# A macaron layer (MoE feed-forward, attention, MoE feed-forward): router banks and the order of scores and value matmuls

## The reference, cut to what matters

```
# feed-forward: 16 routed experts (width 256), all computed densely, and 2 shared ones (width 512)
logits = flat @ router_w                      # 2048 x 16
probs = softmax(logits); weights, idx = top_k(probs, 2); weights /= weights.sum()
comb = sum(one_hot(idx, 16) * weights[..., None], axis=1)
h = silu(flat @ wg_r) * (flat @ wu_r) * comb
out = shared(flat) + einsum('tem,emd->td', h, wd_r)
# attention: 16 heads of 64, with a bias that depends on the relative position
k, v, q = split(x @ w_in, 3)
weights = softmax(q k^T / 8 + bias(rel))
out = (weights v) @ w_gate + b_gate;  return a * sigmoid(g)     # a, g = split(out)
```

## Time and profile before

| what | us |
|---|---|
| two timed runs | 3918.69 and 4110.19 |
| their median, the time before | 4014.44 |
| the profiled execution's own time | 3800.72 |
| its span on the slowest core (core 1) | 3799.1 |
| spans of the eight cores | 3731.9 to 3799.1 |
| TensorE busy | 2845.7 |
| VectorE busy | 1138.8 |
| ScalarE busy | 967.3 |

### The profile page before, as it was taken

The page is one execution under the profiler, slowest core; times in us unless marked ns, Lnnn a source line. Parts: engine busy times, 40 slices in busy tenths (PEclk is TensorE's granted clock), DMA queues, the critical chain, the costliest instruction groups (busy, mean ns, idle before and its releaser), DMA issues. The chain is left out here.

```text
span 3799.1 us, 36293 instructions; the slowest of 8 cores (3731.9 to 3799.1 us)
## 1 busy us (share of the span) xinstructions
PE 2845.7 (75%) x12680; PEld 1215.2 (32%) x12680; DVE 1138.8 (30%) x2460; ACT 967.3 (25%) x987; POOL 172.7 (5%) x265
## 2 busy tenths in 40 slices
PE   0354768999999376767667677656449999999996
PEld 0122324444444222222222222223224444444443
DVE  2521102213031433533534434422433022130320
ACT  2200001101010244645645546531121011010110
POOL 0001110000000001001000001010000000000000
PEclk9577889999999678778778777779859988999888
DMA  3269978556574233223233323222118454564545
GB/s 113 35 114 171 179 171 189 152 170 189 136 180 138 44 48 62 57 53 60 52 54 53 58 46 60 44 33 23 11 42 193 139 158 130 152 186 146 153 127 172
DMA packets 207456, 407.86 MB, mean 107 GB/s; under 512 B 59904, under 2 KB 109312, under 8 KB 207120
## 3 DMA queue, kind: packets, MB, share of 16 engines
q1 hardware_dynamic: 96080, 316.24, 29.8%
q0 software_dynamic: 101968, 52.61, 13.2%
q10 hardware_dynamic: 9232, 36.70, 3.3%
HBM read 405.00 MB, written 40.37 MB: 117 GB/s over the span
## 5 line engine op out<-in xcount | busy, mean ns | idle before, releaser
L560 PE MATMUL f_p<-hf,f_wgu 128*128 128x512 bf16 x2560 | 630.6, 403 | 120.5 <-DMA f_wgu<-wu_r 86.1
L637 PE MATMUL f_p<-f_pall,f_wdb 128*128 128x512 bf16 x2560 | 571.8, 387 | 51.8 <-DMA f_wdb<-wd_r 29.2
L571 PE MATMUL f_p<-hf,f_wgu 128*128 128x512 bf16 x2560 | 607.6, 393 | 0.0
L1098 ACT ACTIVATE at_pexp<-at_ps,at_ngm 128x1024 bf16<-128x1024 f32 x512 | 530.0, 1111 | 181.3 <-PE at_ps L1066 174.0
L1118 DVE TENSOR_TENSOR at_pt<-at_pexp,at_e 128x512 bf16<-128x512 bf16 x1024 | 382.1, 421 | 363.7 <-ACT at_pexp L1098 203.8
L591 ACT ACTIVATE f_gs<-f_p 128x1024 bf16<-128x1024 f32 x160 | 163.7, 1023 | 1110.1 <-PE f_p L560 1110.1
L1046 PE MATMUL at_ppr<-at_pt,at_vtm 128*65 128x512 bf16 x1024 | 372.7, 504 | 83.9 <-DVE at_pt L1118 83.8
L560 PEld LDWEIGHTS f_p<-hf,f_wgu 128*128 128x128 bf16 x2560 | 261.2, 103 | 465.0 <-issue 252.7
L599 DVE TENSOR_TENSOR f_t<-f_p,f_bc 128x1024 f32<-128x1024 f32 x128 | 156.8, 1225 | 740.0 <-PE f_p L571 740.0
L637 PEld LDWEIGHTS f_p<-f_pall,f_wdb 128*128 128x128 bf16 x2560 | 253.1, 99 | 370.7 <-issue 82.3
L571 PEld LDWEIGHTS f_p<-hf,f_wgu 128*128 128x128 bf16 x2560 | 257.1, 100 | 323.8 <-issue 93.5
(11 more groups left out here) (106 smaller groups left out, 1369.6 us busy)
## 6 DMA issues: line engine op xcount, KB each, us to landing
f_wgu<-wbf_scr SPq DMA_DIRECT2D x140, 1024.0 KB, 6.6
f_wdb<-wbf_scr SPq DMA_DIRECT2D x140, 512.0 KB, 3.8
f_bc<-comb_scr SPq DMA_DIRECT2D x128, 256.0 KB, 7.3
wbf_scr<-f_wgu SPq DMA_DIRECT2D x20, 1024.0 KB, 7.6
at_e<-etab_scr SPq DMA_DIRECT2D x32, 608.0 KB, 4.5
at_e<-etab_scr ACTq DMA_DIRECT2D x32, 608.0 KB, 4.5
wbf_scr<-f_wdb SPq DMA_DIRECT2D x20, 512.0 KB, 4.0
xt<-x ACTq DMA_DIRECT2D x1, 8192.0 KB, 39.4
```

Of the source, the lines that this page charges most:

```text
L560: pg=pg, tb=tb: h.matmul(pg[:, mc * 512: mc * 512 + 512], wgu[buf][:, c * 256 + mc * 128: c * 256 + mc * 128 + 128], hf[:, c * S + tb * TB ...
L571: pu=pu, tb=tb: h.matmul(pu[:, mc * 512: mc * 512 + 512], wgu[buf][:, 2048 + c * 256 + mc * 128: 2048 + c * 256 + mc * 128 + 128], hf[:, c ...
L637: mc=mc, po=po, col=col, u=u: h.matmul(po[:, col: col + 512], wdb[buf][:, mc * 1024 + dch * 128: mc * 1024 + dch * 128 + 128], p_all[:, u ...
L1098: hh=h_: h.activation(out=pexp[:, (q % 2) * 2048 + half_i * 1024: (q % 2) * 2048 + half_i * 1024 + 1024], in_=p_s[:, half_i * 1024: half_i ...
```

## The change

In the router the single accumulator becomes four: tile `t` uses bank `t % 4` of `P[0]` and `P[1]`, with columns shifted by 16 for each round of four. The wait of TensorE is then for the copy that was made four tiles earlier in that bank. In attention PV(q-1) is issued behind S(q) for q = 1, 2, 3, and PV(3) alone at the end. `flush_a` stays behind S(1), so PV(0) comes behind it.

```diff
-                ev_prev = None
+                ev_cp = [None] * 4
                 for t in range(NT):
-                    if ev_prev is not None:
-                        ph.wait("tensor", ev_prev)
+                    bk = t % 4
+                    pb = P[bk // 2]
+                    sl = (bk % 2) * 512 + (t // 4) * 16
+                    ph.wait("tensor", ev_cp[bk])
...
-                            P[0][:, 0:16],
+                            pb[:, sl: sl + 16],
...
                                 if q == 1:
                                     flush_a()
-                                if q == 2:
-                                    emit_pv(0)
-                                    emit_pv(1)
+                                if q >= 1:
+                                    emit_pv(q - 1)
...
-                            emit_pv(2)
                             emit_pv(3)
                             flush_b()
```

More of the change, by code:

```diff
@@ L392, in ffn_phase @@
                 pre_issued = first_call
-                ev_prev = None
+                ev_cp = [None] * 4
                 for t in range(NT):
-                    if ev_prev is not None:
-                        ph.wait("tensor", ev_prev)
+                    bk = t % 4
+                    pb = P[bk // 2]
+                    sl = (bk % 2) * 512 + (t // 4) * 16
+                    ph.wait("tensor", ev_cp[bk])
                     for c in range(NDCH):
-                        ph.op("tensor", lambda h, t=t, c=c: h.matmul(
-                            P[0][:, 0:16],
+                        ph.op("tensor", lambda h, t=t, c=c, sl=sl, pb=pb: h.matmul(
+                            pb[:, sl: sl + 16],
                             hf[:, c * S + t * 128: c * S + t * 128 + 128],
@@ L406, in ffn_phase @@
                     ph.wait("vector", ev_mm)
-                    ev_prev = ph.op("vector", lambda h, t=t: h.tensor_copy(
-                        out=lg[:, t * 16: t * 16 + 16], in_=P[0][:, 0:16]),
+                    ev_cp[bk] = ph.op(
+                        "vector", lambda h, t=t, sl=sl, pb=pb: h.tensor_copy(
+                            out=lg[:, t * 16: t * 16 + 16], in_=pb[:, sl: sl + 16]),
                         inc="v")
```

## The result

The changed kernel takes 3686.58 us (median of 11 runs), the kernel before 3779.74 (median of 10, the two of the table above among them). Some executions of either are longer because the cores of one die show a lower clock; they are left out of the ratio, which is 0.977 with a 95% interval of 0.972 to 0.983: 86 us of 3780, between 65 and 106 (so it isn't settled on which side of 2% it lies). The forecast was a gain of 70 us and a time of 3944, between 3830 and 4025. The gain lies in the interval, the time far outside its range. The changed kernel's profiled execution took 3678.8, the old one's 3800.7.

A forecast was written before the change was run, and what follows sets the result against it. No engine is full in attention; a chain of waits sets the pace. Attention 61.6 us, less 5 for the division's trip, plus router 13, gave 70 us off the 4014.4 median: 3944, range 3830 to 4025.

The forecast's parts named there:

- first rival, Full clock through the middle: Attention's clock stays full mid-cycle: early half 11.0 us a cycle, late half 12.4; 116 us saved, 3898; chance 0.15.
- Attention: New PV order: mean cycle 12.43 us against 13.3, 61.6 us saved; some 57 shorter with 5 charged for the division's trip.
- full-clock cycle: Attention cycle laid out at full clock: 0.7 us idle before exp(2)A, no gap before exp(3)A, 11.0 us.
- half-clock cycle: Attention cycle laid out at half clock: 1.7 us idle before exp(2)A, 0.5 before exp(3)A, 12.6 us.
- The mix: Attention: two cycles in three at half clock until S(3) (12.6 us), one with clock up during PV(1) (12.1); mean 12.43.
- Round trip: Attention's division (reciprocal, store, broadcast load, multiplication) becomes level with the shorter cycle late in attention; 5 us charged.
- Router: Both router calls: with four banks a tile takes 0.35 us instead of 0.787; 13 us saved, between 0 and 17.
- All cycles at half clock: Attention cycles all 12.6 us, first ones 12.0, and only 5 us from the router: 50 us saved, 3964; chance 0.17.
- The rule that was weighed there: Skill rule: short pauses between matmul groups make the clock alternate, losing throughput; by it all new attention cycles could be half clock.
- The slower case: Attention: the `at_e` load shares DMA engines with the broadcast load and prolongs the division's trip; +16 us, 4030; chance 0.08.

The follow-up runs named there:

- filled: Changed kernel plus six useless matmuls a cycle (4 behind S(0), 2 ahead of PV(3)); ratio to the kernel before 0.962, attention 1070.8 us.
- div_late: Changed kernel with `flush_b` moved from behind mult(3) to behind mult(0) of the next cycle; ratio to the kernel before 0.974, attention 1119.4 us.
- early_tr: Changed kernel with `flush_a` behind S(0) instead of S(1), `flush_b` behind mult(0) of the cycle after; ratio to the kernel before 0.960, attention 1064.7 us.

## Why the prediction was right or wrong

**The time (wrong).** The step that failed is the sentence "I take the same 70 off the median: 4014.4 - 70 = 3944", and the range behind it. Two runs 190 us apart are no base: eight more of the same kernel lie at 3753 to 3900, and with them the median is 3779.74, 235 us lower. The profiled execution had said so: 3800.7. The sum against that, 3731, is 1.2% from what was measured (3687); the range did not even include it. Nor does the range follow from its own words: half the distance of the two runs is 96 us, and 3898 less 96 and 4005 plus 96 would be 3802 to 4101, which misses 3687 as well. With the profiled time as base the first rival's 116 us would have led to 3685, near what was measured.

**The gain (right in size, in part by luck).** 70 forecast, 65 to 106 measured. The mechanism was right, a long gap before exp(3) traded for a shorter one before exp(2), but errors of its terms offset each other:

- *Attention, 57 for 65.7.* The gap before exp(3) went and a smaller one came before exp(2), as laid out. The full-clock cycle was forecast at 11.0 and is 10.98 (in its sum 4.74 + 2.04 is 6.78 and not 6.76, which changes nothing). The half-clock cycle was forecast at 12.6 and is 13.09: I had counted four PV as 4 x 0.43 = 1.72, and from PV(0) to S(2)A they take 1.85, and again before S(3)A. That is half of the 0.49; in the cycle shown PV(1) also comes 0.97 behind S(2)A where I had 0.86, and I had taken 12.6 for a sum of 12.67. The mix made up for it, and that is luck: I had two cycles in three at half clock until S(3) and none at full, but only 11 to 16 of 56 on a core are 13.0 to 13.4 long and 5 to 12 take 11.0, and the mean is 12.22 instead of 12.43.
- *Round trip, 5 for 14.* The mechanism was right, and VectorE's waits for `at_bca` grew, from 115 to 174 us on the slowest cores. Wrong was its rule of place: I had it bind late in attention, where the trip was 10 us, and said that the late half can't go to 11.0. That was read from core 1; on cores 2, 3, 6 and 7 of the same execution the mean trip is 8.3, early and late. In the changed kernel 10.98 stands in late groups too, and the held cycle shown above is in the third group.
- *Router, 13 for 17.8.* The spacing of 8 matmuls behind a wait (0.22) was the right end of the bound: 0.226. The forecast 0.35 was too careful. The estimate by the Trainium skill ("TensorE: Matmul & The Clock Gate", section "Wait — 56ns, not 53.3ns?"), 62 ns a matmul, is not what these rows show: 28 ns with all the loads of weights between them, at a granted clock of 0.50.

**The rivals.** Full clock through the middle did not come about by the change. Its full-clock cycle of 11.0 was priced right, and filled, where most cycles have it, shows attention 63 us shorter than the changed kernel's. That the late half would be held at 12.4 then was wrong: div_late and early_tr take the hold away, and filled has cycles of 11.0 late as well. All cycles at half clock fell, too: the clock rose from 0.77 to 0.84. The rule that was weighed there (the Trainium skill, "TensorE: Matmul & The Clock Gate", section "A second HAM failure mode: psum-queue depth-cycling") describes what is seen, a clock that goes up and down; the shorter blocks did not make it worse here. The slower case, where the load of `at_e` prolongs the trip, is not ruled out for single cycles: 8 of 448 took more than 14 us, up to 16.5. (By the prediction's own loop a trip of 14 makes a cycle of 16.3, not 16.5.) In each of the 43 held cycles on the eight cores that load ran beside the broadcast load for over 2 us, but a late trip meets it whatever made it late. The store ahead of it, which hardly met that load, was longer too, 3.2 us against 2.1 in the cycles that are not held (the broadcast load 6.0 against 4.3). So the load of `at_e` is not all of it; how much it is was not tried.

## What to carry to other kernels

When a block of matmuls is split so that the next scores come earlier, count what else stands ahead of them: here four transposes of 0.56 us together cost a cycle 0.5 us at full clock and more through the clock, and moving them to where TensorE waits anyway (early_tr beside div_late) took another 55 us off attention, where the change had taken 66. Where the clock alternates within a cycle, lay the cycle out at both levels: the same order was worth 10.98 and 13.09. And a saving that is worked out from a profile belongs on the profile's own time; a median of two runs that lies 6% above it needs a range that holds both.

## What the runs showed of the hardware

- Useless matmuls can pay: 384 more of them (108 us of busy time by the profile) made attention 63 us shorter, while the granted clock rose from 0.84 to 0.91.
- 128 matmuls of 16 columns, each with its own weights, run at 28 ns apiece for 3.5 us at a granted clock of 0.50, with four banks and a copy behind each eight (the changed kernel's first router).
- The round trip reciprocal, store, broadcast load, multiplication varies between 6.6 and 11.7 us in one execution (core 7 of the changed kernel), so single cycles are held (12 of 56 on that core) where the mean trip of 9.1 would not do it. Cores 0 and 1, 2 and 3, 4 and 5, 6 and 7 have nearly the same mean trip, the pairs differ by up to 1.7 us.
- On cores 0 and 1 of one execution (the kernel before) the clock stood at 0.81 for two stretches of 160 us of dense matmuls, while cores 2 and 3 of the same die had 0.99 or 1.00. That stage took 961 us on them and 902 to 908 on the others.
